# Sums over gathered table rows: rows as the moving operand, weights in four column tiles of the TensorE array

## The reference

```python
scores, idx = jax.lax.top_k(sim, PK_TOPK)
index = (idx0[..., :, None] + idx1[..., None, :]).reshape(b, n, HEADS, PK_TOPK * PK_TOPK)
final_scores, pk_idx = jax.lax.top_k(score, FINAL_TOPK)
final_scores = jax.nn.softmax(final_scores, axis=-1)
k = jnp.einsum('bnhk,bnhkd->bnhd', kv_scores, keys_table[ind])
v = jnp.einsum('bnhk,bnhkd->bnhd', kv_scores, values_table[ind])
sim = jnp.einsum('bihd,bjhd->bhij', q, k)
attn = jax.nn.softmax(sim, axis=-1)
out = jnp.einsum('bhij,bjhd->bhid', attn, v)
```

## Time and profile before

| | |
|---|---|
| time, median of 3 runs | 12402.95 us (12400.67 to 12414.53) |
| profiled execution, first to last instruction | 12361.9 us, granted TensorE clock 0.985 |
| PE busy | 11555.1 us, 93% |
| DVE busy | 10243.6 us, 83% |
| ACT busy | 7855.1 us, 64% |
| POOL busy | 8371.1 us, 68% |
| parts: L1042, PE | 16384 passes, 2114.1 us busy |

### The profile page before, as it was taken

One profiled execution on the slowest core, in us unless ns is written; L12 is line 12 of the kernel. 1 busy time (PEld: TensorE's weight loads), 2 busy tenths in 40 slices (PEclk: granted clock), 3 DMA queues, 4 the chain that ended last, 5 costly groups with the idle time before them and its releaser, 6 DMA issues.

```text
span 12361.9 us, 263881 instructions
## 1 busy us (share of the span) xinstructions
PE 11555.1 (93%) x70396; PEld 8975.2 (73%) x70396; DVE 10243.6 (83%) x42179; ACT 7855.1 (64%) x17926; POOL 8371.1 (68%) x8196
## 2 busy tenths in 40 slices
PE   3999999999999999999999999999999999999999
PEld 2777777777777777777777777777777777777777
DVE  6888888888888888888888888888888888888883
ACT  2666666666666666666666666666666666666665
POOL 0667666676676676676776766766767667667676
PEclk6999999999999999999999999999999999999999
DMA  2556555555555565555555555655555555555554
GB/s 65 154 166 174 150 166 166 156 170 163 160 171 156 164 173 152 167 168 152 170 162 161 171 156 163 175 150 168 162 156 171 158 161 172 151 166 170 156 166 135
DMA packets 1651836, 1975.58 MB, mean 160 GB/s; under 512 B 336238, under 2 KB 1125870, under 8 KB 1649902
## 3 DMA queue, kind: packets, MB, share of 16 engines
q1 hardware_dynamic: 1387950, 1418.48, 39.0%
q0 software_dynamic: 262144, 537.40, 16.3%
HBM read 1881.20 MB, written 73.40 MB: 158 GB/s over the span
## 4 chain that ended last, share of the span: by engine, by line
PE 69%; ACT 10%; DVE 9%; issue 6%; DMA 4%; SPq 1%; ACTq 0%; DVEq 0%
PE bank L1006 18%; PE bank L1042 11%; PE bank L1029 7%; PE bank L1016 6%; ACT bank L1253 4%; PE bank L889 4%; PE bank L993 3%; DMA moving<-keyspace 3%; PE bank L936 3%; PE bank L970 2%; PE bank L1066 2%; PE bank L1060 2%; PE bank L1058 2%; ACT decay L1194 2%; ACT weight L1260 2%
## 5 line engine op out<-in xcount | busy, mean ns | idle before, releaser
L817 POOL DMA_INDIRECT gath<-in_table_dram,rowsT x8192 | 8370.9, 1022 | 3960.4 <-issue 2456.6
L1260 ACT ACTIVATE weight<-bank 128x512 f32<-128x512 f32 x4096 | 2442.5, 596 | 3172.6 <-PE bank L1016 3155.7
L1006 PE MATMUL bank<-weight,rowtab 128*128 128x256 f32 x16384 | 4248.5, 381 | 0.0
L1006 PEld LDWEIGHTS bank<-weight,rowtab 128*128 128x128 f32 x16384 | 3110.3, 191 | 750.6 <-issue 27.3
L1253 ACT ACTIVATE bank<-bank,seventeen 128x512 f32<-128x512 f32 x4096 | 2714.5, 663 | 14.6 <-PE bank L1016 11.6
L1042 PEld LDWEIGHTS bank<-spread,gath 128*128 128x128 f32 x16384 | 2162.5, 193 | 135.4 <-issue 13.8
L1042 PE MATMUL bank<-spread,gath 128*128 128x96 f32 x16384 | 2114.1, 273 | 0.0
L1029 PE MATMUL bank<-moving,pick_b 96*128 96x512 bf16 x4096 | 1583.2, 387 | 476.4 <-ACT bank L1253 400.7
L1016 PE MATMUL bank<-moving,pick_b 96*128 96x512 bf16 x4096 | 1557.6, 380 | 41.5 <-DMA moving<-keyspace 40.8
L1572 DVE TENSOR_TENSOR_SCAN decay<-decay,wide 128x256 f32<-128x256 f32 x2048 | 1238.7, 670 | 0.3
L1029 PEld LDWEIGHTS bank<-moving,pick_b 96*128 96x128 bf16 x4096 | 420.3, 103 | 914.3 <-ACT bank L1253 768.1
(11 more groups left out here) (257 smaller groups left out, 16932.7 us busy)
## 6 DMA issues: line engine op xcount, KB each, us to landing
rowtab<-in_tableD_dram SPq DMA_DIRECT2D x2048, 256.0 KB
wide<-states SPq DMA_DIRECT2D x512, 512.0 KB
moving<-keyspace SPq DMA_DIRECT2D x4096, 64.0 KB
gath<-in_table_dram,rowsT POOLq DMA_INDIRECT x8192
moving<-keyspace SPq DMA_DIRECT2D x4096, 32.0 KB
pix<-in_x_dram SPq DMA_DIRECT2D x504, 256.0 KB
keyspace<-split SPq DMA_DIRECT2D x256, 256.0 KB
out_dram<-acc SPq DMA_DIRECT2D x64, 64.0 KB
```

The lines of the kernel that those rows point to most:

```text
L817: pool.indirect_dma_start(out=gath[:, u % RING, j, :], out_offset=None, in_=table, in_offset=bass.IndirectOffsetOnAxis(ap=rowsT[k][:, col: ...
L1006: mm(dense_ps[:, 0:TOK], rowtab[:, r, s % 2 * 2 + half, :], weight[s % 2][:, half * TOK:(half + 1) * TOK], start=(s % 16 == 0 and half == ...
L1260: ins = af(weight[s % 2][:], zd_ps[s % 2][:], ACT.Exp, scale=-1.0)
```

## The change

- The operands change sides. A matmul's weights are no longer streamed. Its stationary operand is 32 columns of `spread`, of which 8 hold weights of a part's quarter and 24 are zero, and the gathered rows are streamed, 128 columns. Its result is tokens on 32 partitions by 128 channels.
- The four matmuls of a part write PSUM partitions 0 to 31, 32 to 63, 64 to 95 and 96 to 127, so they stand in four column tiles of the array. Four parts are added up into the same place (`start` at v = 0, `stop` at v = 3); where the 8 columns stand among the 32 goes with v. GpSimd gathers columns in the order that goes with this.
- Since tokens are on partitions now, ACT copies the head to `gsum` (new item k, `keep_sums`), PE transposes it in two matmuls (new item h, `turn_sums`), and ACT makes `kvg` from the result (item c, the former k).
- `spread` has two buffers instead of four, so wb1, wb2 and wb3 stand later in DVE's table.
- In PE_ORDER a part stands one slot earlier: in slots 0, 2, 4, ... instead of 1, 3, 5, ...

Each line below moves one slot's row as an example; in the tables all 32 parts move so.

```diff
-STREAM = 96
+TURN = 32
+MARGIN = 24
...
-16 z15+0 o16+0 d14+0
-17 z16+0 d15+0 o17+0 g1.0+0 a7.6-1
+16 z15+0 o16+0 d14+0 h0+0 g1.0+0
+17 z16+0 d15+0 o17+0 a7.6-1
...
-0 w63-1 l0+0 k3-1 a5.5-1 F.sq2+2 F.sq3+2 S.E2+0
+0 w63-1 l0+0 c3-1 a5.5-1 F.sq2+2 F.sq3+2 S.E2+0
...
-16 w15+0 l16+0 a7.5-1 F.rs0+2 k0+0
-17 w16+0 l17+0 K0+0
+15 w14+0 a7.4-1 F.kv10+2 F.kv11+2 l15+0 k0+0
+16 w15+0 l16+0 a7.5-1 F.rs0+2
+17 w16+0 c0+0 l17+0 K0+0
...
-32 w31+0 l32+0 k1+0 a1.5+0 K1+0
+31 w30+0 F.rs1+2 l31+0 k1+0
+32 w31+0 l32+0 a1.5+0 K1+0 c1+0
...
-                        col = g * SPAN + u % 8 * PART + j
+                        col = g * SPAN + u % 8 // 4 * 16 + 4 * j + u % 4
...
             def gather_sums(b, g, i):
-                u = 8 * g + i
+                u, half, v = 8 * g + i, i // 4, i % 4
                 pe.wait_ge(gathered[u % RING], ...)
                 if i == 0:
                     pe.wait_ge(spread_ready, b * GH + g + 1)
-                    wait(pe, kept_g, b * GH + g)
+                    wait(pe, summed_g, b * GH + g)
                 for j in range(PART):
-                    col = (i * PART + j) * 8
-                    flat = spread[g][:].rearrange("p i c -> p (i c)")
-                    mm(sums_ps[:, col:col + STREAM], gath[:, u % RING, j, :],
-                       flat[:, col:col + STREAM], start=True, stop=True)
+                    at = MARGIN + (16 * half + 4 * j + v) * TURN - 8 * v
+                    mm(sums_ps[j * TURN:(j + 1) * TURN, half * P:(half + 1) * P], spread[g % 2][:, at:at + TURN],
+                       gath[:, u % RING, j, :], start=(v == 0), stop=(v == 3), skip_group_check=True)
+            def turn_sums(b, g):
+                pe.wait_ge(summed_g, b * GH + g + 1)
+                wait(pe, kept_g, b * GH + g)
+                pe.sem_inc(held, 1)
+                for half in range(2):
+                    pe.transpose(sums_ps[:, TOK + half * P:TOK + (half + 1) * P], gsum[:, half * P:(half + 1) * P], ident[:])
...
+            def keep_sums(b, g):
+                if g > 0:
+                    act.wait_ge(slot_step, seen(b, f"h{g - 1}"))
+                elif not isinstance(b, int) or b > 0:
+                    wait(act, slot_step, seen(b + (-1), f"h{GH - 1}"))
+                act.wait_ge(slot_step, seen(b, part_name(8 * g + 7)))
+                af(gsum[:], sums_ps[:, 0:TOK], ACT.Copy).then_inc(summed_g, 1)
             def keep_gathered(b, g):
...
-                act.wait_ge(slot_step, seen(b, part_name(8 * g + 7)))
-                af(kvg[:].rearrange("p (c i) -> p c i", c=8), sums_ps[:, 0:TOK].rearrange("p (i c) -> p c i", c=8),
+                act.wait_ge(slot_step, seen(b, f"h{g}"))
+                af(kvg[:].rearrange("p (c i) -> p c i", c=8), sums_ps[:, TOK:2 * TOK].rearrange("p (i c) -> p c i", c=8),
                    ACT.Copy).then_inc(kept_g, 1)
...
-                v.tensor_tensor(spread[g][:, 0:SPAN, :], src, own[:].unsqueeze(1).to_broadcast([P, SPAN, 8]),
+                dst = spread[g % 2][:, MARGIN:].rearrange("p (i c) -> p i c", c=TURN)[:, :, 0:8]
+                v.tensor_tensor(dst, src, own[:].unsqueeze(1).to_broadcast([P, SPAN, 8]),
```

More of the change, by code:

```diff
@@ new lines @@
+12 z11+0 o12+0 d10+0 g0.6+0 a7.3-1
+13 z12+0 o13+0 d11+0 S.s2+1 F.kv9+2 F.kv10+2
+14 z13+0 o14+0 d12+0 g0.7+0 F.kv11+2
+15 z14+0 o15+0 d13+0 a7.5-1 S.s3+1
+16 z15+0 o16+0 d14+0 h0+0 g1.0+0
+17 z16+0 d15+0 o17+0 a7.6-1
+18 z17+0 o18+0 d16+0 g1.1+0 a0.0+0 F.t0+2
+19 z18+0 o19+0 d17+0 F.q+2
+20 z19+0 o20+0 d18+0 g1.2+0 a0.3+0
+21 z20+0 o21+0 d19+0
+22 z21+0 o22+0 d20+0 g1.3+0
+23 z22+0 o23+0 d21+0 a0.5+0
+24 z23+0 o24+0 d22+0 g1.4+0
+25 z24+0 o25+0 d23+0 a0.6+0
+26 z25+0 o26+0 d24+0 g1.5+0 a1.0+0
@@ new lines @@
+27 z26+0 o27+0 d25+0
+28 z27+0 o28+0 d26+0 g1.6+0 a1.3+0
+29 z28+0 o29+0 d27+0 F.t1+2
+30 z29+0 o30+0 d28+0 g1.7+0 F.pj+2
+31 z30+0 o31+0 d29+0 a1.5+0
+32 z31+0 o32+0 d30+0 h1+0 g2.0+0
+33 z32+0 d31+0 o33+0 a1.6+0 F.t2+2
+34 z33+0 o34+0 d32+0 g2.1+0 a2.0+0 S.A0+1 F.xz+2
+35 z34+0 o35+0 d33+0
+36 z35+0 o36+0 d34+0 g2.2+0 a2.3+0
+37 z36+0 o37+0 d35+0
+38 z37+0 o38+0 d36+0 g2.3+0 S.A1+1
+39 z38+0 o39+0 d37+0 a2.5+0 F.xd+2 F.dt+2
+40 z39+0 o40+0 d38+0 g2.4+0
+41 z40+0 o41+0 d39+0 a2.6+0 S.E0+1
+42 z41+0 o42+0 d40+0 g2.5+0 a3.0+0
@@ new lines @@
+43 z42+0 o43+0 d41+0
+44 z43+0 o44+0 d42+0 g2.6+0 a3.3+0
+45 z44+0 o45+0 d43+0 S.E1+1
+46 z45+0 o46+0 d44+0 g2.7+0
+47 z46+0 o47+0 d45+0 a3.5+0
+48 z47+0 o48+0 d46+0 h2+0 g3.0+0
+49 z48+0 d47+0 o49+0 a3.6+0
+50 z49+0 o50+0 d48+0 g3.1+0 a4.0+0
+51 z50+0 o51+0 d49+0
+52 z51+0 o52+0 d50+0 g3.2+0 a4.3+0
+53 z52+0 o53+0 d51+0
+54 z53+0 o54+0 d52+0 g3.3+0
+55 z54+0 o55+0 d53+0 a4.5+0 F.S0+2
+56 z55+0 o56+0 d54+0 g3.4+0 F.S1+2
+57 z56+0 o57+0 d55+0 a4.6+0 F.S2+2
+58 z57+0 o58+0 d56+0 g3.5+0 a5.0+0 F.S3+2 S.A2+1
@@ L190 @@
 46 w45+0 l46+0 a3.4+0
-47 w46+0 l47+0 F.dc3+2
-48 w47+0 l48+0 k2+0 F.dc4+2 a3.5+0 K2+0
+47 w46+0 l47+0 F.dc3+2 k2+0
+48 w47+0 l48+0 F.dc4+2 a3.5+0 K2+0 c2+0
 49 w48+0 l49+0
@@ L214 @@
 3 F.h2+1 S.re3+0
-4
+4 S.wb1+0
 5 a6.3-1 S.n0+1 S.n1+1 S.lo3+0 S.R7+0
@@ L245 @@
 34 S.G2+1
-35 F.uz0+2 S.G3+1 S.re0+1
+35 S.wb3+0 F.uz0+2 S.G3+1 S.re0+1
 36
@@ L273 @@
 62 S.R4+1 S.lo2+1 S.R5+1
-63 S.wb1+1 S.R6+1
+63 S.R6+1
 """
@@ L543, in build @@
         rowsT = [sb(f"rowsT{k}", [P, GH * SPAN], U32) for k in range(2)]
-        spread = [sb(f"spread{g}", [P, SPAN + STREAM // 8 - 1, 8]) for g in range(GH)]
+        spread = [sb(f"spread{k}", [P, MARGIN + SPAN * TURN]) for k in range(2)]
+        gsum = sb("gsum", [P, TOK])
         acc = [sb(f"acc{k}", [P, TILES, C]) for k in range(2)]
@@ L1372, in prepare @@
                 step(v.memset(ones64, 1.0 / C))
-                for g in range(GH):
-                    step(v.memset(spread[g][:, SPAN:, :], 0.0))
+                for k in range(2):
+                    step(v.memset(spread[k][:], 0.0))
                 step(v.memset(seventeen[:], 17.0 * BIG))
```

100 lines of the change are left out of this document (30 added, 70 removed).

## The result

The changed kernel takes 12543.38 us (median of 4 runs, 12531.15 to 12561.13) against 12401.81 (12387.99 to 12414.53) before: ratio 1.0121, 95% interval 1.0104 to 1.0139. The profiled execution spans 12534.4 us at a granted TensorE clock of 0.967 (before 12361.9 at 0.985). The change costs 142 us where 280 were forecast: slower, as predicted, and by half as much. How it got there is not how the prediction said.

What follows compares the result with a forecast made beforehand. PE (93% busy) was taken as pace-maker, though not in every slot. Part -4.9, new steps +1.8 and moved cover +7.5 gave +4.4 us an image, +280 over 64 images: 12,403 to about 12,690 us, own range 12,520 to 12,850.

Steps and rivals of the forecast that it cites:

- The part: Eight PE passes of a gather part: 0.57 us, 0.71 with switches, against 0.86 before; -4.9 us an image.
- 5 rounds: PE, inside a part: only one tile's second pass and the next tile's first overlap; 5 x 0.109 + 0.025 = 0.57 us.
- rival (b): Parts on PE: tiles overlap fully, a part with switches costs 0.39 us; -2.4 us an image, 12,250 us; chance 0.18.
- Rival (a): Parts on PE: column tiles don't overlap at all; +15.0 us an image, 13,350 us, range 13,150 to 13,450; chance 0.22.
- Switches: PE around each part: 0.093 us per change of array shape, 48 an image; 4.5 us an image, 0.14 a part.
- Turns: New transposes on PE (L1053), two, four times an image: 4 passes of 0.109, 0.44 us each time; +1.8 us an image.
- The cover of the odd slots: Odd slots the parts leave: what of the 0.86 isn't got back to floors and waits; 15.5 us an image with slot 1.
- the even slots: Even slots the parts enter: what of the part vanishes in waits; 7.9 us an image, leaving net cover +7.5.
- DVE's floor: Slots 40 to 63, as next bound if parts are cheap: can give at most 1.7 us an image, 0.9 taken.
- Slot 1: ACT's copy c3 waits for slot 1's overs: slot grows about 1.3 us instead of losing 0.86; 2.1 us an image.
- Its clock: PE's longer stand in slot 1 may also cost granted clock: net cover 9 us an image instead of 7.5.
- The sum: Whole kernel: -4.9 + 1.8 + 7.5 = +4.4 us an image, +280 over 64 images, about 12,690 us, 2.3% slower.

Runs made afterwards that it cites:

- e8: The changed kernel with the four matmuls of a part in one column tile instead of four; 13471.9 us, ratio to the kernel before 1.0866.
- e7: The changed kernel plus five f32 matmuls of 128x384, results unread, in PE's slot 1 wait; 12531.51 us, ratio to the kernel before 1.0106.
- e5: The changed kernel with ACT's copy c3 moved between slot 1's weights and over-limit copy; 12340.93 us, ratio to the kernel before 0.9939.
- e3b: The changed kernel with parts and turns back in the old odd slots, ACT's k and c one slot later; 12200.88 us, ratio to the kernel before 0.9829.
- e10: The changed kernel, parts in old odd slots but seven one slot ahead, plus unread matmuls in PE's slot 1 waits; 12149.16 us, ratio to before 0.9801.

## Why the prediction was right in sign and half in size

- **The part: "5 rounds", 0.57: wrong.** The step that failed is the one by which the two passes of one matmul stand behind each other, so that only neighbours overlap. The windows show two rounds of four; the records don't say which pass of which matmul stands in which round. A part takes 0.36 with its exit switch, so 0.26 of its own; with 0.14 for switches 0.40, against 0.86: -14.6 us an image where I took -4.9. That is rival (b)'s term. The chance given to it was 0.18, and the reason against it ("the two passes depend on each other") came from no row. The Trainium skill, "TensorEngine Tiling (Array Packing)", Key Properties, says that different tiles can load weights and multiply in parallel; the trace agrees. The rule of the Trainium skill, "TensorE: Matmul & The Clock Gate", Part 3, that loads overlap running matmuls only when the row group differs, doesn't hold here: these tiles share all rows, and eight loads and four passes overlap in the windows above.
- **The price of no overlap: right.** Rival (a) said 0.90 and 0.093 a part and 13,350 us; e8 has 0.99 with the exit switch and takes 13,472, just above that rival's range (13,150 to 13,450); its slots 2 to 4 hold falls of the clock that (a) didn't count.
- **Switches: right.** 0.09 on the product ahead and 0.093 behind.
- **Turns: too dear by half.** I counted four f32 passes, 0.44. The row of L1053 has x2: a transposition is one pass, 0.31 with the switch, 0.9 us an image and not 1.8. The earlier trace rows had it: L1071 is three transpositions, and x3.
- **The cover of the odd slots: right in most rows.** Slot 21 has 1.90 with 1.46 busy, 43 still 2.32, 55 4.14, 33 3.27. In the means slots 15, 19 and 49 keep their length within 0.01, and 23 keeps 0.27 of 0.86. It was wrong for 53, which gave all of its 0.86 and not 0.26, for 39 and 51, which gave 0.24 and 0.36 and not 0.16, and in the last slots (next point). With a part of 0.40 the even slots hide less of it (at most 0.40 each where I had up to 0.86: 5.8 instead of 7.9), so cover would be +9.7.
- **DVE's floor: left out of the forecast, and named only in rival (b).** I let slots 57, 59, 61 and 63 give all of their 0.86; in the means 57 does, 59 and 63 give 0.63 and 0.57, and 61 grows by 0.47. Slot 61 of the 25th image is 4.17 us with DVE 4.07. By my list with the corrected sizes slots 40 to 63 should have given 2.5 us an image (parts -5.5, turn +0.2, cover +2.8); in the means they take 75.01 against 74.76. That DVE is what took it is read off its busy share, no run tested it.
- **Slot 1: the wait right, the clock too small.** Forecast: grows by 1.3, above 5 us, ACT idle over 1 us. Measured in the mean 1.57, in the row 6.43 and 1.63. Its clock was a remark at the upper end of a bound, 1.5 us for the case that it should fall; it falls in the slots behind, in each of the 45 middle images, and e7 prices it at 3.0.
- **The sum.** -14.6 + 0.9 + 9.7 + 3.0 = -1.0, and 2.7 not had in slots 40 to 63: +1.7. The runs show +2.2 (142 / 64), but the middle images, from which the terms are taken, +3.4. So 1.7 us an image of the middle ones stays unassigned, 0.5 of it in slots 0 to 4 and 1.2 in slots 5 to 39. The forecast of 4.4 was near because a gain too small by 10.6 met losses too small by 7.9: slot 1 and the cover, which carry the sign, were right as mechanisms, but that they outweigh the part holds only with the clock and slots 40 to 63, which were not in the sum. Sign and size were luck in part.
- **The alternative that I had not priced.** e5 shows the sign hanging on the place of one copy, and e3b that with the parts kept in the slots of before the same matmuls make the kernel 1.7% faster than before.

## What to carry to other kernels

When an instruction gets one more producer ahead of it (here the turn), look up where the waiting engine sees that producer in program order, and what is queued behind the wait: here it was 3.2 us of ACT's copies and squares, and their lateness turned a gain of 0.6% (e5) into a loss of 1.2%. Price a stand of PE twice, once as time and once as clock for the slots behind it; filling the stand with streams that nobody reads can be worth it (0.6% in e10), but size them by the row of the same data type. And before work is taken out of a slot, ask what the slot's length is without it: two thirds of the odd slots here had a floor, or waits, that the work had been covering.
